# A graph network step on Trainium2: the first step's dense products dealt evenly over its 25 chunks

## The reference, cut to what matters

```python
def step(h, _):
    messages = h[col] @ W_msg.T + b_msg
    agg = segment_sum(messages, row, num_segments=num_nodes)
    gi = agg @ W_ih.T + b_ih
    gh = h @ W_hh.T + b_hh
    i_r, i_z, i_n = split(gi, 3); h_r, h_z, h_n = split(gh, 3)
    r = sigmoid(i_r + h_r); z = sigmoid(i_z + h_z)
    n = tanh(i_n + r * h_n)
    return (1.0 - z) * n + z * h, None
```

## Time and profile before

| | |
|---|---|
| median of 3 runs | 5297.94 us (5295.67 to 5298.79) |
| the profiled execution: first to last instruction (span) | 5295.2 us; the page gives no other time of its own |
| TensorE matmul busy | 4969.6 us, 94% |
| GpSimd busy | 3751.4 us, 71% |
| VectorE busy | 2590.3 us, 49% |
| ScalarE busy | 861.8 us, 16% |
| mean granted TensorE clock | 0.975 |

### The profile page before, as it was taken

The page is one execution under the profiler, slowest core; times in us unless marked ns, Lnnn a source line. Parts: engine busy times, 40 slices in busy tenths (PEclk is TensorE's granted clock), DMA queues, the critical chain, the costliest instruction groups (busy, mean ns, idle before and its releaser), DMA issues. The chain is left out here.

```text
span 5295.2 us, 80372 instructions
## 1 busy us (share of the span) xinstructions
PE 4969.6 (94%) x26501; PEld 2539.4 (48%) x26502; DVE 2590.3 (49%) x6993; ACT 861.8 (16%) x1421; POOL 3751.4 (71%) x3869
## 2 busy tenths in 40 slices
PE   5588888699999699999999999999999999999998
PEld 1344444355555345555555555555555555555554
DVE  8899993356666633433333433333343333333332
ACT  7666662000000000000000000000000000000000
POOL 3777777777776777677777677777767777757774
PEclk7799999899999799999999999999999999999999
DMA  5255555466666466666676666666666667566654
GB/s 170 68 165 164 164 165 167 118 183 183 175 174 173 114 195 182 185 181 181 176 203 179 183 180 181 180 188 192 178 184 181 181 179 212 177 182 188 189 177 125
DMA packets 1036729, 916.12 MB, mean 173 GB/s; under 512 B 507905, under 2 KB 771453, under 8 KB 1036412
## 3 DMA queue, kind: packets, MB, share of 16 engines
q1 hardware_dynamic: 482262, 661.95, 40.1%
q0 software_dynamic: 123920, 212.72, 15.0%
q10 hardware_dynamic: 430358, 39.09, 6.0%
HBM read 766.27 MB, written 147.15 MB: 172 GB/s over the span
## 5 line engine op out<-in xcount | busy, mean ns | idle before, releaser
L696 POOL DMA_INDIRECT f_ring<-fast_hrows,f_work x3175 | 3070.9, 967 | 1208.7 <-issue 950.6
L990 PE MATMUL f_ps_a<-f_ring,f_hr 128*128 128x512 fp8e4 (+1 forms) x13560 | 3017.1, 375 | 6.9 <-DMA f_ring<-fast_adj 6.9
L990 PEld LDWEIGHTS f_ps_a<-f_ring,f_hr 128*128 128x128 f16 x13560 | 1308.2, 98 | 1473.8 <-issue 138.2
L1500 DVE TENSOR_SCALAR f_ring<-f_iota_h,f_work 128x128 f16<-128x128 f16 (+1 forms) x3175 | 614.0, 283 | 1026.8 <-PE f_ps_a L1002 984.8
L674 POOL DMA_INDIRECT fast_rec<-f_slots x656 | 645.1, 983 | 213.7 <-issue 199.6
L1002 PE MATMUL f_ps_a<-f_ring 128*128 128x128 f16 (+1 forms) x5726 | 542.7, 237 | 62.9 <-DMA f_ring<-fast_hrows,f_work 62.7
L1424 DVE SCALAR_TENSOR_TENSOR f_work<-f_deg,f_bias_c,f_ps_c 128x512 f32<-128x512 f32 x125 | 93.5, 748 | 1009.8 <-PE f_ps_deg L1029 1009.8
L1002 PEld LDWEIGHTS f_ps_a<-f_ring 128*128 128x128 f16 x5726 | 440.8, 98 | 260.8 <-DMA f_ring<-fast_hrows,f_work 68.1
L792 ACT ACTIVATE f_work<-f_work,f_bsum 128x512 f32<-128x512 f32 x125 | 90.2, 722 | 2223.4 <-DVE f_work L1424 2223.4
L1374 DVE TENSOR_SCALAR f_ring<-f_iota_h,f_work 128x256 f16<-128x256 f16 x1536 | 413.2, 373 | 0.0
L949 PE MATMUL f_ps_deg<-f_ring,f_sel 128*128 128x512 fp8e4 x1536 | 395.6, 381 | 0.0
(11 more groups left out here) (322 smaller groups left out, 3164.3 us busy)
## 6 DMA issues: line engine op xcount, KB each, us to landing
f_ring<-fast_adj SPq DMA_DIRECT2D x750, 640.0 KB, 4.2
fast_adj<-f_ring SPq DMA_DIRECT2D x192, 512.0 KB, 3.2
f_ring<-fast_hrows,f_work POOLq DMA_INDIRECT x3175
f_deg<-fast_deg SPq DMA_DIRECT2D x125, 256.0 KB
fast_hrows<-f_work ACTq DMA_DIRECT2D x400, 64.0 KB
f_hr<-fast_hrows SPq DMA_DIRECT2D x24, 640.0 KB, 7.1
fast_rec<-f_slots POOLq DMA_INDIRECT x656, 2.4
fast_hrows<-f_deg SPq DMA_DIRECT2D x1, 6528.0 KB, 39.4
```

The source lines that it names most:

```text
L696: nc.gpsimd.indirect_dma_start(G[:, g * 2 * H:(g + 1) * 2 * H], None, hrows, bass.IndirectOffsetOnAxis(ap=idx_tab[:, col + g:col + g + 1], ...
L990: mm = pe.matmul(sumT[buf][:, 0:cols], lhsT=hr[:, t, a * H:(a + 1) * H], rhs=a_f8[:, t * CHUNK:t * CHUNK + cols], start=(t == 0 and a == 0 ...
L1500: ins = nc.vector.tensor_scalar(OH[:, g * HALF:g * HALF + w], iota_h[:, 0:w], loc[:, bass.ds(col + g, 1)], HOT, ALU.is_equal, ALU.mult)
```

## The change

The three chunks ahead stay. What is left, 22 x 60 dense tiles, is dealt over the 25 bodies: `first_tiles(q, t)` gives the dense tiles for slot t of body q, 22/25 of one on average, so 52 or 53 per body. The lead is 3 chunks in body 0 and 0 at the end of body 24. SP's program is written out in the same order as TensorE's. A chunk's first dense tile now waits for the bank's last sum itself (`s_ready`), in place of a wait at each body's start. Since a chunk's dense part may now end in its own body, the closes wait for `dense_done` in the first step too. Steps 1 to 4 are as before.

```diff
@@ -529,6 +529,13 @@
         LAST = STEPS * NCH - 1
+        LATER = NCH - LEAD
+
+        def first_tiles(q, t):
+            begin = q * T1 + t
+            return [divmod(LEAD * T1 + n, T1) for n in range(begin * LATER // NCH, (begin + 1) * LATER // NCH)]
...
@@ -599,20 +606,23 @@
                 def first_step():
 
-                    for d, (cls, k) in enumerate(FIRST_STEP):
+                    def unit_taken(d, u):
+                        sp.wait_ge(dense_done, d * UNITS + u + 1)
+                        sp.sem_inc(sp_turns, 1)
+                        load_a(u, chunk_of(*(FIRST_STEP[d + 1] if d + 1 < NCH else first_chunk(1))))
+                        if d == NCH - 1:
+                            reload_rows(0, u)
+
+                    for d in range(LEAD):
                         for u in range(UNITS):
-                            sp.wait_ge(dense_done, d * UNITS + u + 1)
-                            sp.sem_inc(sp_turns, 1)
-                            load_a(u, chunk_of(*(FIRST_STEP[d + 1] if d + 1 < NCH else first_chunk(1))))
-                            if u == 4 and d >= LEAD:
-                                first_degrees(d - LEAD)
-                    first_degrees(NCH - 3)
-                    for u in range(4):
-                        reload_rows(0, u)
-                    first_degrees(NCH - 2)
-                    reload_rows(0, 4)
-                    first_degrees(NCH - 1)
-                    reload_rows(0, 5)
+                            unit_taken(d, u)
+                    for q in range(NCH):
+                        for t in range(T1):
+                            if t == 5 * UT - 1:
+                                first_degrees(q)
+                            for d, at in first_tiles(q, t):
+                                if at % UT == UT - 1:
+                                    unit_taken(d, at // UT)
...
@@ -810,8 +820,7 @@
                     if cls == "C":
                         if s == 0:
                             act.wait_ge(set_done[SETS["C"] - 1], uses("C", 0, k, SETS["C"] - 1) + 2)
-                        else:
-                            act.wait_ge(dense_done, q * UNITS + UNITS)
+                        act.wait_ge(dense_done, q * UNITS + UNITS)
...
@@ -1043,6 +1052,8 @@
                 def first_dense(d, t):
 
+                    if t == 0 and d >= len(sumT):
+                        pe.wait_ge(s_ready, d - len(sumT) + 1)
                     if t % UT == 0:
                         dense_unit_loaded(d, t // UT)
...
@@ -1057,7 +1068,6 @@
                         gates_of_h(q - 1, c, s)
-                        pe.wait_ge(s_ready, q)
                     for t in range(T1):
...
@@ -1067,8 +1077,8 @@
-                        if q + LEAD < NCH:
-                            first_dense(q + LEAD, t)
+                        for d, at in first_tiles(q, t):
+                            first_dense(d, at)
...
@@ -1481,8 +1491,7 @@
                     if s == 0:
                         dve.wait_ge(set_done[SETS[cls] - 1], uses(cls, 0, k, SETS[cls] - 1) + 2)
-                    else:
-                        dve.wait_ge(dense_done, q * UNITS + UNITS)
+                    dve.wait_ge(dense_done, q * UNITS + UNITS)
```

More of the change, by code:

```diff
@@ L531, in build_fast @@
         LAST = STEPS * NCH - 1
+        LATER = NCH - LEAD
+        def first_tiles(q, t):
+            begin = q * T1 + t
+            return [divmod(LEAD * T1 + n, T1) for n in range(begin * LATER // NCH, (begin + 1) * LATER // NCH)]
+        assert all(d >= q and d - q <= LEAD for q in range(NCH) for t in range(T1) for d, _ in first_tiles(q, t))
         block = mem.enter_context(nc.Block())
```

## The result

The changed kernel takes **5254.66 us**, median of 4 runs (5253.84 to 5256.02), beside 5297.54 us for the kernel before (5295.67 to 5298.79). The ratio is 0.992 with a 95% interval of 0.9907 to 0.9933. That is 42.9 us less, where 35 were forecast (5263, range 5247 to 5282). The profiled execution has a span of 5252.9 us beside 5295.2, 42.3 less.

The account below looks back on a forecast made before the run. TensorE was taken as the bound until its dense work ran out, then the gathers. 32.1 + 1.3 + 1.2 = 34.6 us off the 5295.2 span gave 5260.6, plus 2.7 for the median: 5263, range 5247 to 5282.

Parts of the forecast that it names:

- Step 1: Full bodies of the first step: 7 fewer dense tiles cut TensorE's work from 35.08 to 32.06 us, below GpSimd's need.
- Step 2: Bodies 1 to 20 go at GpSimd's gather pace c, taken as 33.5 us a chunk, between 32.58 and 34.50.
- rival B: Bodies 1 to 20: gathers collide at every update and one-hot sum, c 34.0 to 34.5, 5273 to 5283 us; chance 0.16.
- Rival A: Bodies 1 to 20: gathers run nearly free of collisions, c of 32.6 to 32.9, 5245 to 5251 us; chance 0.14.
- Step 3: Start of body 21: chunk 21's first gather, S(21), at 1673.2 us, the body starting 3.8 later.
- Steps 4 and 5: Bodies 21 to 24: 22.8 us, then 32.06 each; the second step starts at 1797.2, 32.1 us earlier.
- Step 6: Seam to the second step: 1.3 us back as TensorE no longer arrives cold, 1.2 from a gather wait going.
- Step 7: Reload of the rows at the seam, moved s_ready wait, SP's order, dense_done wait: covered, counted as nothing.
- a stall at the reload of the rows: At the seam to the second step: listed as a sign that the prediction is wrong, no size given.
- C: First step: waits for gathers lower TensorE's clock and bodies grow; slower, 5319 us at a mean of 0.90; chance 0.03.
- D: Class A chunks: VectorE becomes the bound, eating the gain at 1.7 us in each of 20 bodies, 5298; chance 0.04.
- E: Bodies that follow the gathers: one-hots block gathers, c = 37.4, gain -43, 5341 us; chance 0.01.

Follow-up runs that it names:

- narrow: The changed kernel with five VectorE operations on two fp32 SBUF inputs cut to 8 of 512 columns in the first step; 5244.38 us.
- startwait: The changed kernel with the wait for s_ready put back at each body's start in the first step; 5254.18 us.
- short: The changed kernel without one of the two matmuls of every sixth dense tile in the first step; 5249.92 us.
- stt: The changed kernel with five VectorE tensor_tensor operations written as scalar_tensor_tensor with a scalar of 1.0; 5254.17 us.

## Why the prediction was right

It was right in its mechanism, and the time lies in its range; the measured gain is 42.9 us where it had 34.6. Step by step:

- **Step 1**, a full body of 32.06 us. Where TensorE waits for nothing the gate products stand exactly that far apart: those of chunks 6, 7 and 8 come at 1216.86, 1248.92 and 1280.97.
- **Step 2**, the pace c. Here is the error, a term that was mis-sized: 33.5 taken, 33.09 measured, 20 x 0.41 = 8.2 us. The bounds held it. I averaged five chunks that were coupled to TensorE, and two of them (34.50 and 33.89) came from the bodies without dense work, where TensorE was cold and idle; rival B's own argument said that they stood apart. The other three average 33.04. What moves c, gathers that begin under an operation with two SBUF inputs, was the right cause: narrow takes them away and c is 32.60. Rival A's phase without collisions did not settle, nor did B's: the 520 gathers from S(1) to S(21) have 44 long ones (over 1.04 us), about two a chunk.
- **Step 3**: S(21) = 1002.53 + 20 x 33.09. The start was 0.6 earlier than before.
- **Steps 4 and 5**: body 21 was forecast at 22.8 us. From its gate product to the next is 24.86, a stretch that holds parts of two bodies; the next two intervals are 32.05 and 32.06. Measured from one L1021 to the next it took 23.67, 0.9 more than forecast, and TensorE waited once for summed degrees, 0.58 us, where three waits of 0.4 were counted; the two misses nearly cancel. GpSimd lost 3.1 us at class B, forecast "some 3". The second step began at S(21) + 124 by the forecast, its G(24) 8.5 later at S(21) + 132.5; it came at S(21) + 132.3. This part of the sum is right to 0.2 us, a little of it by that luck.
- **Step 6**, 2.5 us at the seam: the first part came, since G(24) follows 8.5 us behind the step's beginning. The second, 1.2 us, did not. The wait for a gather did go, as said, but in its place stands one of 1.58 us for the reload of the rows, and the interval is 36.60 (36.53 before).
- **Step 7** is where that wait was passed over: "no stall", by the look of the seam between steps 1 and 2. That one does not carry over: here the last reload took 7.4 us to land, and TensorE asked for it 6.0 after its issue. The prediction had named "a stall at the reload of the rows" as a sign of being wrong; it came, at 1.58 us. The rest of step 7 held: s_ready is worth nothing either way (startwait), and no wait for an adjacency unit shows.

The account closes: 34.6 forecast, + 8.2 for c, + 0.6 for the earlier start, - 1.2 at the seam = 42.2, against 42.3 between the spans.

**The rivals.** C, the clock: TensorE waits 17 times for a gather between 1003 and 1664 us, 21.4 us in all, and its granted clock over the stretch is 0.99, the same as before. Short makes that 39 waits and 44.7 us, the longest 2.73, and the clock is 0.98. So even twice as much waiting lowers the mean clock by a hundredth only. The loss sits in short spells at the lower of the clock's two levels, each behind a wait, and the longest wait of the changed kernel shows one. TensorE's timeline at the start of body 6, and the stretches ahead of it and behind:

```profile
1206.04 0.40 PE L1011 MATMUL f_ps_b<-f_ring 128*128 128x128 f16 x4 [4.37 <-DMA f_ring<-fast_hrows,f_work]
1206.27 1.55 PE L999 MATMUL f_ps_a<-f_ring,f_hr 128*128 128x512 fp8e4 x4
1207.62 1.92 PE L1021 MATMUL f_ps_c<-f_hT,f_whhT 128*128 128x512 f32 x2
```

```profile
1192.00:1200.00 8.00, 8.00 (x47) 4.06 (x45) 7.97 (x26) 0.00 (x0) 5.87 (x8) 1.00 1.00 207
1206.00:1214.00 8.00, 7.96 (x31) 3.70 (x32) 1.29 (x3) 0.60 (x1) 6.06 (x7) 0.79 0.35 92
```

Behind 4.37 us of waiting the mean clock of 8 us is 0.79: the two products of L1021 took 1.92 us where they take 1.02, and a few groups behind them were slow too. The body's gate interval is 38.29, and the next bodies, at 32.06, 32.05 and 32.22, took it back, since GpSimd was not held up. A wait need not be that long. Behind one of 2.35 us (1660.24) the mean clock of the changed kernel is 0.79 again, from 1660.2 to 1668.2, while behind one of 2.30 (1003.12) it is 1.00. In short six waits of 1.94 to 2.73 us are each followed by 8 us with a mean of 0.79, the one of 2.38 at 1564.16 for example:

```profile
1564.00:1572.00 8.00, 7.84 (x34) 3.89 (x35) 1.76 (x7) 0.00 (x0) 5.87 (x8) 0.79 0.45 125
```

The Trainium skill (TensorE: Matmul & The Clock Gate, "HAM oscillation — how this bites in real kernels") warns of being throttled again at every tile; this trace shows it behind two of the seventeen waits, and short behind six of thirty-nine. Why these waits and not others of the same length is not shown. So C had a real mechanism at a small price: the slack under the gathers took it up.

D, no change: no wait of TensorE for VectorE's close held a body to 35. E, the one-hots blocking gathers: fallen, 111 gathers beginning under L1509 last 0.957 us on average and 1.01 at most. The Trainium skill (GPSIMD Engine Reference, "Specifications") names two-port instructions and instructions with two SBUF inputs as contention for the interfaces that VectorE and GpSimd share. Of the second kind the traces agree, for two fp32 inputs (248 of 248 gathers) and for an fp32 and an f16 one (1.12 us in narrow). Of the first kind no run says which operations it holds for. If the one-hots are it, only 0.015 us a gather shows, and each of them is short (20 in 3.77 us); the tensor_scalar of 0.43 us in narrow, with one SBUF input, did make its gather last 1.17.

## What to carry to other kernels

Where a scarce engine is the bound in some stretches and idle in others, and another engine is the reverse, count the work per stretch that makes both equally slow, and deal the movable work so: a lead that is all used up early gives the second engine a surplus that its buffers can't hold, and it is lost just before it is needed. When an engine is to follow another, price it at that engine's pace in stretches where both are busy and warm, not where the follower was starved. And look at each transfer near a seam again once the seam moves: a load that was covered before has less time now.

## What the runs showed of the hardware that was not expected

- A gather's issue on GpSimd lasts 0.94 us. When it begins 0.05 to 0.5 us into a VectorE operation of 0.69 us on two tiles in SBUF, it ends 1.50 to 1.52 us behind that operation's beginning, and so lasts up to 1.46: with tensor_tensor and scalar_tensor_tensor alike (stt), with two fp32 inputs and with an fp32 and an f16 one (1.12 in narrow). Beside operations with one input in PSUM it stays under 0.96. At 20 chunks this is 10 us (narrow).
- To say that an operation leaves gathers alone, one has to see gathers begin inside it. L1460 seemed harmless in twelve of the thirteen traces because none ever did.
- TensorE had 0.98 of its clock in a stretch of 659 us with 39 waits of up to 2.73 us (short). The loss came behind six of them, of 1.94 to 2.73 us, each with a mean of 0.79 over the 8 us that follow; in the changed kernel it came behind one of 4.37 and one of 2.35, and not behind one of 2.30.
- The wait of 4.37 us is for a gather issued at 1198.58, some 7.5 us before, in a stretch where the DMA engines were busy for a share of 1.00 (1192 to 1200). Whether they caused it was not tested.
